# Turning the quantized rows of an FFN by transposing transfers, with the work of ScalarE and VectorE shared out anew

## The reference

```
patches = unfold(ln_c(x), 3)                    # 16384 patches of 96 channels x 9 positions
y = cosine(patches, w_mask)                     # against 512 prototypes, best (prototype, position) picked
h = leaky_relu([mixed row, 9 similarities] @ w_i1.T + b_i1)
vcs = tanh(h @ w_i2.T + b_i2)
h1 = relu(vcs @ w_l1.T + b_l1)
x = x + fold(conv(h1 @ w_l2.T + b_l2))          # t: 147456 tokens of 96 channels

tn = (t - mean(t)) / sqrt(var(t) + 1e-5)        # _ln_t, over the 96 channels of a token
hid = relu(q_acc(q_mul(tn) @ q_mul(W1).T) + q_mul(b1))     # 384 hidden values
out = t + q_acc(q_mul(hid) @ q_mul(W2).T) + q_mul(b2)      # q_mul: 8-bit float, q_acc: 16-bit float
```

## Time and profile before

| | |
|---|---|
| time, median of 3 runs | 2088.41 us (2086.51 to 2092.78) |
| the profiled execution, its own time | 2092.94 us |
| its span, first to last instruction | 2090.8 us |
| mean granted TensorE clock | 0.981 of full speed |
| busy: PE / DVE / ACT / POOL | 94% / 96% / 87% / 74% |

### The profile page before, as it was taken

One profiled execution on the slowest core, in us unless ns is written; L12 is line 12 of the kernel. 1 busy time (PEld: TensorE's weight loads), 2 busy tenths in 40 slices (PEclk: granted clock), 3 DMA queues, 4 the chain that ended last, 5 costly groups with the idle time before them and its releaser, 6 DMA issues.

```text
span 2090.8 us, 46997 instructions
## 1 busy us (share of the span) xinstructions
PE 1957.4 (94%) x13105; PEld 1434.5 (69%) x13105; DVE 2003.2 (96%) x6781; ACT 1829.2 (87%) x5381; POOL 1549.9 (74%) x1042
## 2 busy tenths in 40 slices
PE   5899999999999999999999999999999999999975
PEld 4677777777777777767777777777777777777653
DVE  7999999999999999999999999999999999999953
ACT  1179999999999999999999999999999999999997
POOL 2577877878778777787887777878778778787753
PEclk9999999999999999999999999999999999999985
DMA  3322232332322323323233232232332322323111
GB/s 89 97 78 88 94 106 87 98 102 87 108 91 95 105 87 102 97 91 110 86 97 103 87 107 92 95 105 87 102 97 93 108 86 98 103 87 111 46 40 51
DMA packets 65475, 193.27 MB, mean 92 GB/s; under 512 B 13689, under 2 KB 15939, under 8 KB 65219
## 3 DMA queue, kind: packets, MB, share of 16 engines
q1 hardware_dynamic: 52866, 170.80, 25.2%
q0 software_dynamic: 10240, 18.89, 3.0%
q10 hardware_dynamic: 2112, 0.60, 0.1%
HBM read 133.23 MB, written 57.02 MB: 91 GB/s over the span
## 4 chain that ended last, share of the span: by engine, by line
DVE 89%; issue 6%; PE 3%; ACT 1%; POOL 0%; DMA 0%; POOLq 0%; ACTq 0%; DVEq 0%
DVE best_y L1026 28%; DVE h L1043 13%; DVE stats L1035 9%; DVE t_pm L1051 6%; DVE simraw L1077 6%; DVE top_v L1065 4%; DVE w_index L1072 4%; DVE zb L992 3%; DVE xn L984 1%; DVE mix_in L971 1%; DVE m_dif L929 1%; DVE r_u L1010 1%; DVE ra L1018 1%; DVE one_j L903 1%; DVE r_t L1015 1%
## 5 line engine op out<-in xcount | busy, mean ns | idle before, releaser
L1026 DVE TENSOR_REDUCE best_y<-y_ps 128x2 f32<-128x1024 f32 (+1 forms) x640 | 692.7, 1103 | 4.0 <-PE y_ps L651 3.9
L466 ACT CAST y<-bank 128x384 f16<-128x384 f32 x1152 | 550.5, 478 | 140.8 <-PE bank L674 129.8
L649 PE MATMUL y_ps<-proto_hi,xh 96*128 96x512 f32 x1152 | 553.8, 481 | 22.2 <-DVE best_y L1026 10.4
L359 POOL TENSOR_TENSOR tq<-t_dev,ra 128x864 fp8e5<-128x864 f32 x128 | 209.5, 1637 | 401.3 <-DVE ra L1018 401.3
L650 PE MATMUL y_ps<-proto_lo,xh 96*128 96x512 f32 x1152 | 458.4, 398 | 0.0
L651 PE MATMUL y_ps<-proto_hi,xl 96*128 96x512 f32 x1152 | 457.3, 397 | 0.0
L475 ACT ACTIVATE h<-h 128x1152 fp8e5<-128x1152 f16 x384 | 448.3, 1168 | 0.0
L674 PE MATMUL bank<-tqt,f_w 96*128 96x384 f16 x1152 | 390.4, 339 | 26.5 <-ACT y L466 24.6
L403 POOL TENSOR_TENSOR xl<-xc,xh 96x1152 fp32r<-96x1152 f32 x128 | 339.7, 2654 | 26.4 <-ACT xh L536 15.2
L1043 DVE TENSOR_SCALAR h<-y,f_b 128x1152 f16<-128x1152 f16 x384 | 306.1, 797 | 21.0 <-ACT y L466 20.9
L505 ACT ACTIVATE sq_junk<-t_dev 128x96 f32<-128x96 f32 x1152 | 318.8, 289 | 0.9 <-POOL t_dev L371 0.9
(11 more groups left out here) (131 smaller groups left out, 3997.3 us busy)
## 6 DMA issues: line engine op xcount, KB each, us to landing
xc<-x_cm SPq DMA_DIRECT2D x128, 432.0 KB, 4.0
xp<-x_pm SPq DMA_DIRECT2D x128, 432.0 KB, 4.8
out<-o_pm SPq DMA_DIRECT2D x128, 432.0 KB, 2.5
xsel<-x_pm,x_index POOLq DMA_INDIRECT x128, 2.5
wsel<-proto_rows,w_index POOLq DMA_INDIRECT x128, 4.9
proto_rows<-proto SPq DMA_DIRECT2D x1, 384.0 KB, 2.6
proto<-w_mask SPq DMA_DIRECT2D x1, 192.0 KB, 3.4
f_f<-w_1t ACTq DMA_DIRECT2D x1, 144.0 KB
```

What stands on the lines that cost most here:

```text
L466: act.copy(y16[:, q, r, 0:TOK], bank[0][:, 0:TOK]).then_inc(s_y16, 1)
L649: pe.matmul(y, hi, proto_hi[:], start=True, stop=False)
L1026: dve.tensor_reduce(best_y[t % 2][:, j0:j1], y_ps[n % 2][:, 0:j1 - j0, :], AX_X, ALU.max).then_inc(s_yd, 1)
```

## The change

The change has four parts.

1. The nine transposes of `turn` on TensorE and the two copies `turned` on ScalarE go. In their place SP issues nine transposing transfers in each slot, from `tq` in SBUF to `tqt` in SBUF, 128x128 values of 16 bits each (`tq` is widened from 96 to 128 columns for each of the nine positions). They are issued once `tq` is there; the first `ffn1` of the next slot waits for all nine.
2. The nine operations of `squares` become one Square over all 864 values, into `t_sq`, and VectorE sums it by one `tensor_reduce`, `t_squares`, at the start of the next slot.
3. The three `ffn_bias` of a tile move from VectorE to ScalarE, as `hidden16`: a Relu with the bias.
4. The lists of all four engines are written in another order.

```
@@ sync, slot(s), between the loads and the store
+                if run.live(s, NORM):
+                    t = s - NORM
+                    run.wait(s_tq, t + 1)
+                    run.wait(s_f1, NC * (t - 1))
+                    for j in range(J):
+                        sp.dma_start(tqt[t % 2][:, j * P:(j + 1) * P], tq[t % 2][:, j, :],
+                                     transpose=True).then_inc(s_tt[t % 2], 16)
@@ gpsimd, t_norm
-                    run.wait(s_tf, 2 * (t - 1))
+                    if t >= 2:
+                        run.wait(s_tt[t % 2], 16 * J * (t // 2))
@@ gpsimd, slot(s)
+                gather_x(s)
                 lock(s)
                 t_norm(s)
                 product(s)
                 t_center(s)
-                gather_x(s)
+                low_x(s)
                 output(s)
-                low_x(s)
                 low_h(s)
                 gather_w(s)
@@ scalar
+            def hidden16(s, stage, q):
+                if run.live(s, stage):
+                    t = s - stage
+                    run.wait(s_y16, NC * t + 3 * (q + 1))
+                    run.wait(s_h8, NH * (t - 1) + q + 1)
+                    run.apart()
+                    act.activation(h16[:, q, :, 0:P].rearrange("p (r j) l -> p r j l", r=3),
+                                   y16[:, q, :, 0:TOK].rearrange("p r (j l) -> p r j l", l=P), ACT.Relu,
+                                   bias=f1_b[:, q:q + 1]).then_inc(s_h16[q], 1)
-            def turned(s, n):
...
-                    act.copy(tqt[t % 2][:, j0 * P:j1 * P], bank16[3 - n][0:C, 0:(j1 - j0) * P]).then_inc(s_tt, 1)
-            def squares(s, js):
...
+            def squares(s):
                 if run.live(s, CONV):
                     t = s - CONV
+                    run.wait(s_dev, t + 1)
+                    run.wait(s_sqd, t)
+                    run.apart()
+                    act.activation(t_sq[:], t_dev[t % 2][:], ACT.Square).then_inc(s_sq, 1)
@@ tensor
-            def turn(s, n):
...
-                        last = pe.transpose(bank16[3 - n][0:C, (j - j0) * P:(j - j0 + 1) * P],
-                                            tq[t % 2][:, j * C:(j + 1) * C], ident16[:])
...
             def ffn1(s, k):
...
                     if k == 0:
-                        run.wait(s_tt, 2 * (t + 1))
+                        run.wait(s_tt[t % 2], 16 * J * (t // 2 + 1))
@@ vector
+            def t_squares(s):
+                if run.live(s, NORM):
+                    run.wait(s_sq, s - NORM + 1)
+                    ins = dve.tensor_reduce(va[s % 2][:, J:2 * J], t_sq[:].rearrange("p (j c) -> p j c", c=C), AX_X, ALU.add)
+                    ins.then_inc(s_sqd, 1)
@@ vector, slot(s)
+                x_dif(s)
+                t_squares(s)
                 low_part(s)
...
-                ffn_bias(s, FFN2, 2)
...
-                ffn_bias(s, FFN, 0)
...
-                ffn_bias(s, FFN, 1)
```

More of the change, by code:

```diff
@@ L155, in build @@
         t_pm = [sb(f"t_pm{b}", [P, JC]) for b in range(RING)]
-        tq = [sb(f"tq{b}", [P, JC], F16) for b in range(2)]
-        tqt = [sb(f"tqt{b}", [C, JP], F16) for b in range(2)]
+        tq = [sb(f"tq{b}", [P, J, P], F16) for b in range(2)]
+        tqt = [sb(f"tqt{b}", [P, JP], F16) for b in range(2)]
         y16 = sb("y16", [P, NH, 3, TOK + 8], F16)
@@ L212, in build @@
         s_tq = sem("tq_ready")
-        s_tf = sem("tqt_filled")
-        s_tt = sem("tqt_ready")
+        s_tt = [sem(f"tqt_turned{b}") for b in range(2)]
         s_f1 = sem("ffn1_filled")
         s_y16 = sem("y16_ready")
-        s_h16 = sem("h16_ready")
+        s_h16 = [sem(f"h16_ready{q}") for q in range(NH)]
         s_h8 = sem("h8_ready")
@@ L471, in hidden8 @@
                     t = s - stage
-                    run.wait(s_h16, NH * t + q + 1)
+                    run.wait(s_h16[q], t + 1)
                     run.wait(s_f2, 2 * (t - 1))
@@ L565, in slot @@
             def slot(s):
+                high(s)
                 ffn1_out(s, 0)
+                hidden8(s, FFN2, 1)
+                ffn1_out(s, 1)
                 vcs_out(s)
-                ffn1_out(s, 1)
-                hidden8(s, FFN2, 1)
-                high(s)
+                hidden16(s, FFN2, 2)
                 ffn1_out(s, 2)
+                xnt_out(s)
                 hidden8(s, FFN2, 2)
-                xnt_out(s)
                 ffn1_out(s, 3)
+                hidden16(s, FFN, 0)
                 layer1_out(s)
                 mix_out(s)
+                ffn1_out(s, 4)
                 weighted(s)
-                turned(s, 0)
-                ffn1_out(s, 4)
-                turned(s, 1)
-                hidden1_out(s)
[L582 to L588, removed]
+                hidden8(s, FFN, 0)
+                ffn1_out(s, 5)
+                ffn2_out(s, 0)
+                ffn1_out(s, 6)
+                squares(s)
+                ffn1_out(s, 7)
+                hidden1_out(s)
+                hidden16(s, FFN, 1)
+                ffn1_out(s, 8)
                 ffn2_out(s, 1)
-                squares(s, range(4, 7))
-                ffn1_out(s, 8)
-                squares(s, range(7, 9))
             run.slots(slot)
@@ L759, in slot @@
             def slot(s):
+                match(s, 0)
+                ffn1(s, 0)
+                match(s, 1)
                 hidden2(s)
-                ffn1(s, 0)
-                match(s, 0)
                 ffn1(s, 1)
@@ L765, in slot @@
                 ffn1(s, 2)
-                match(s, 1)
+                turn_x(s)
                 conv(s, 1)
                 match(s, 2)
-                turn_x(s)
+                ffn1(s, 3)
                 match(s, 3)
-                ffn1(s, 3)
+                turn_mix(s)
                 layer1(s)
-                turn_mix(s)
-                turn(s, 0)
+                match(s, 4)
                 ffn1(s, 4)
-                turn(s, 1)
-                hidden1(s)
[L778 to L783, removed]
+                match(s, 5)
+                pick(s)
+                ffn2(s, 0)
+                ffn1(s, 5)
+                match(s, 6)
+                ffn1(s, 6)
+                match(s, 7)
+                ffn1(s, 7)
+                hidden1(s)
+                match(s, 8)
                 ffn2(s, 1)
-                match(s, 6)
-                ffn1(s, 7)
-                match(s, 7)
                 ffn1(s, 8)
-                match(s, 8)
             run.slots(slot)
@@ L954, in variances @@
                     if run.live(s, NORM):
-                        run.wait(s_sq, s - NORM + 1)
+                        run.wait(s_sqd, s - NORM + 1)
                         run.apart()
```

57 lines of the change are left out of this document (18 added, 39 removed).

## The result

| | before | after |
|---|---|---|
| time, median | 2090.2 us (4 runs) | 2422.75 us (4 runs, 2415.41 to 2426.15) |
| ratio after / before | | 1.1588, 95% interval 1.1554 to 1.1621 |
| span of the profiled execution | 2090.8 us | 2420.2 us |
| mean granted TensorE clock | 0.981 | 0.89 |
| a slot: span / 136 | 15.37 us | 17.80 us |

A forecast was written before the change was run, and what follows sets the result against it. VectorE's list was taken to bound the 15.38 us slot; ScalarE's new 14.71 plus 0.15 for gaps gives 14.85. Over 128 slots 68 us come off 2092.9, giving 2025, forecast as a 2021 us median, range 1990 to 2160.

The forecast's parts named there:

- What bounds the kernel before: VectorE's list, without gaps, sets the slot of 15.38 us; TensorE and ScalarE follow it.
- The list of ScalarE: ScalarE's work per slot goes from 14.18 to 14.71 us, the longest of the new lists.
- The single relu: On ScalarE, each of three new relu operations a slot takes 1.07 us to the next start, 3.21 in all.
- The rival in which ScalarE keeps its 1.2 us of waits: ScalarE bounds at 15.91 us a slot, 2156 us, chance 0.10; with half the waits kept, no gain, 0.08.
- The list of VectorE: Three bias operations go (2.16 us) and a sum comes (0.96), so VectorE's slot falls from 15.38 to 14.18 us.
- 0.15 us for gaps between TensorE and ScalarE: Allowance per slot for places where the two lists don't fit, as between `ffn1` 1 and 2.
- The pace of the transfers: SP issues the nine transposing transfers 0.6 us apart, hidden up to a pace of 0.8 us each.
- D: Time from `tq` ready to the landing of the ninth transfer, forecast at 7.3 us.
- the dear end: On SP's queue each transfer starts only when the one ahead has landed: 9 x 2.5 = 22.5 us, time 2890.
- My estimate from that page: Nine transfers following each other at the skill's 1309 ns: D 13.0 us, slot 16.9 us, some 2280 us.
- The rival of late transfers: TensorE stands at the first `ffn1`; two slots share the lateness, slot 14.85 + (D - 8.9)/2; 2110 us at gather's pace; chance 0.22.
- the room of 8.9 us: Time counted from `tq` ready (7.4 us) until TensorE's waiting first `ffn1` (16.36 us), for the transfers to land.

The follow-up runs named there:

- the fastest variant: The changed kernel with one transposing transfer a slot instead of nine, and `x_dif` moved from the slot's head to behind `low_part`: 1999.4 us, ratio 0.9559.

## Why the prediction was wrong

**What bounds the kernel before** was right. The transfer alone relieves the two other engines and gains only 0.2%.

**The list of ScalarE** came out at its sum, partly by luck: I had 14.71, and the fastest variant, which it bounds, has slots of 14.70. The single relu was undersized (1.27 us open where I expected 1.17, and in that variant 1.15 us from its start to the next where I took 1.07, so 0.24 a slot; the Square, at 0.93, and the sum, at 1.04, came as expected), and the other steps together took that much less. The rival in which ScalarE keeps its 1.2 us of waits was wrong: its idle time did come from VectorE's lead.

**The list of VectorE** was 14.18 by my sum and 14.96 in the run without transfers. Of the 0.78 between them 0.6 is `x_dif`, which steps 1207.46 - 1206.79 = 0.67 us where it took 0.08 before: what I left out was that the new order puts a two-input operation beside GpSimd's `output`. The other 0.2 lies in small steps that I can't assign. The slot that I forecast without late transfers, 14.85, was close to the measured 14.95 by luck: I had 0.15 us for gaps between TensorE and ScalarE, and they weren't there, while VectorE's list was longer by more than that.

**The pace of the transfers** is the step that failed: "I take 0.6 us each: D = 8 x 0.6 + 2.5 = 7.3 us, hidden with 1.6 us to spare." They are issued 1.27 us apart, the ninth lands 2.3 us after its issue, and D is 12.4 us. Of the bounds 0.43 and 2.5 I chose by SP's plain load, and held that only the gather's 0.98 spoke for more; the true pace lies between that and the dear end. The Trainium skill (VectorE: DVE Perf Modes, the three transpose paths) gives 1309 ns for one 128x128 transfer, and I set this aside because its figure for TensorE didn't fit five transposes in a row. The trace agrees with it as a pace: nine in a row start 1.27 us apart, though the landing of one takes longer than that. My estimate from that page, some 2280 us, was nearer than my forecast, and still 140 us short. That TensorE's figure seemed to be of one operation alone said nothing about SyncE's.

**The rival of late transfers** was right in its mechanism and its place: TensorE stands at the first `ffn1`, the lateness falls on every second slot, and it turns slower than before at a pace below the measured one. At D = 12.4 its rule gives 14.85 + (12.4 - 8.9)/2 = 16.6 us. Measured were 36.19/2 = 18.1 in the round shown, 17.8 over the span. Two terms were missing. One is the clock. After the wait for the transfer TensorE runs at the lower of its two levels, 1.2 GHz: from the first `ffn1` to the start of `match` 2 it takes 1447.36 - 1440.86 = 6.50 us, and the same list in the kernel with one transfer 1211.13 - 1206.73 = 4.40. That is 2.1 us of every two slots.

```profile
1440.86 0.48 PE L666 MATMUL bank<-tqt,f_w 96*128 96x384 f16 x1 [5.45 <-DMA tqt<-tq]
...
1447.36 0.39 PE L653 MATMUL y_ps<-proto_hi,xh 96*128 96x512 f32 x1
...
1435.50:1440.86 5.36, 0.00 (x0) 0.03 (x1) 4.15 (x27) 1.17 (x2) 2.55 (x4) 0.91 0.23 52
1440.86:1446.59 5.73, 5.73 (x20) 4.63 (x20) 0.30 (x1) 3.42 (x5) 3.34 (x2) 0.50 0.93 247
1446.59:1450.00 3.41, 3.41 (x21) 2.77 (x19) 2.95 (x6) 3.27 (x6) 1.31 (x1) 0.99 0.14 25
```

```profile
1206.73 0.34 PE L666 MATMUL bank<-tqt,f_w 96*128 96x384 f16 x1
...
1211.13 0.39 PE L653 MATMUL y_ps<-proto_hi,xh 96*128 96x512 f32 x1
...
1208.00:1211.00 3.00, 2.97 (x17) 2.06 (x16) 3.00 (x20) 3.00 (x6) 0.99 (x1) 1.00 0.90 288
```

(The first fence is of the changed kernel, the second of the one with one transfer: the timeline, then windows, whose last three figures are granted clock, DMA share and GB/s.) The granted clock starts to fall while TensorE stands idle (0.91 over the wait), is 0.50 for the next 5.73 us, and then back. The transfers that run in that stretch are not what slows the matmuls: with one transfer the DMA share is as high, 0.90 against 0.93, at a granted clock of 1.00. That the low clock is caused by the wait is read from the rows; no run tested it by itself.

The other is that the room of 8.9 us was too large. My rule puts together a round of 14.2 us from the first `ffn1` to the end of the last drain, 4.4 to the end of the roots, 2.1 to the end of `tq`, and 12.4 for the transfers, 33.1 in all. In the round shown these are 16.4, 4.6, 2.6 and 12.4, and 0.2 more pass from the landing to the `ffn1`: 36.2. So 2.2 us more lie ahead of the last drain's end, where the low clock costs its 2.1, and 0.9 behind it, which is room that I didn't have. Half a microsecond of it is the gather that the change moved to the head of GpSimd's list:

```profile
1461.87 0.94 POOL L351 DMA_INDIRECT xsel<-x_pm,x_index  x1 [5.62 <-DVE x_index L888]
1462.84 1.64 POOL L368 TENSOR_TENSOR tq<-t_dev,ra 128x864 fp8e5<-128x864 f32 x1
```

The roots are done at 1461.74 + 0.14 = 1461.88, when the gather has only begun, so `tq` starts 0.96 us after them where I had 0.2 + 0.3. It is so in 27 of the 28 slots from 1000 to 1500 us. Why the gather begins no sooner, with its index written at 1461.03, the rows don't show, and no run moved it back. With both terms the rule gives 16.6 + 2.1/2 + 0.9/2 = 18.1 us. The run with six transfers speaks for the smaller room too: its slot of 2100.5/136 = 15.44 us at D = 8.7 asks for a room of 7.7 by the rule, from the 14.95 without transfers and with no term for the clock.

The range was also cut wrongly. A slot at its end of 2160 us has (2160 - 2021)/128 = 1.1 us more than my forecast, which is D = 11.1 and a pace of 1.07 us; I had written 1.15. The measured pace lies outside either way.

**SyncE's queue** I took to have nothing else to do. It has: the load of `xp` behind the nine is wanted in its own slot. In the change this is hidden behind the larger wait, and with a slot more for the transfers it comes out.

## What to carry to other kernels

A transposing transfer here costs its queue about 1.27 us, whether it turns 128x128 or 128x1152 values; so give one instruction all the blocks, and count instructions before bytes. A set of transfers that has to land within a stage needs its issue pace times their count, plus the landing, and everything that stands behind it in the queue needs the same look. And when work moves between engines, the gain is what the longest of the new lists allows, and only if each part is there; two halves that bring nothing or lose alone brought 2.4% together, and 4.4% once one small operation was taken out of GpSimd's way.

## What the runs showed of the hardware that was not expected

- Nine transposing transfers of 32 KB held SyncE's queue for 11.7 us, three of 96 KB for 3.8, one of 288 KB for 1.3. The Trainium skill (DMA: Bandwidth & Descriptors, rules for kernel authors) asks to coalesce many small transfers into a large one; here the nine were 387 us slower than the one.
- A VectorE operation with two inputs in SBUF, `x_dif`, stayed open until GpSimd's operation on SBUF had ended (0.74 us for 9 columns); operations with one input beside it, such as the last drain (0.68 us), kept their duration. This is what the Trainium skill states (SBUF — State Buffer, who interferes with whom: "A DVE instruction with two SBUF inputs contends with a GpSimd instruction that reads SBUF"). The run with the move, 0.15 us and 37 us less in all, agrees.
- After a wait of about 5 us TensorE ran at half speed (granted clock 0.50) for some 6 us. In the run with the later `ffn1` a wait of 2.15 us and more waits behind it were followed by about 10 us of it.
